# Runs of eight product groups between reductions, in place of four, in a pairwise-interaction kernel

## The chip, the cores and the metric

The kernel runs on one core of a Trainium2 chip. TensorE does the matrix products and writes PSUM, VectorE multiplies, ScalarE copies and applies biases, GpSimd starts gathers, and SyncE starts the large loads. The metric is device time in microseconds (us); lower is better. Before the change the median of three runs is 269.88 us (267.64 to 270.34).

## The reference

512 samples each carry 32 integer ids. Each id picks a row of 64 values from its own table, so a sample becomes 32 vectors of 64. For each of the 496 pairs of fields i < j there is a 64x64 matrix, and the pair's value is a bilinear form:

```
rows, cols = np.triu_indices(32, k=1)
pij = einsum('bpe,dpe,bpd->bp', e[:, rows], kernel, e[:, cols])
z = pij @ W.T + b                                  # 496 -> 256
h = relu(concat([z, dense_ctx]) @ W_top1 + b_top1) # 272 -> 512
h = relu(h @ W_top2 + b_top2)                      # 512 -> 256
y = h @ W_top3                                     # 256 -> 1
```

Everything is fp32.

## The kernel before, in words

**Data.** The 32 fields are paired into 16 chunks. A chunk lies in `x_sb` as 128 partitions (two fields of 64 values) by 512 samples. The rows of the first three chunks are picked with one-hot matrices. For the other 13 GpSimd gathers eight blocks of 128 rows a chunk (L258, 104 gathers in all, each held back until the one two before it has landed, L255 to L257), and TensorE turns each gathered chunk with four transposes (`turn`, L295 to L304, matmuls L303). ScalarE copies the turned chunk out (L450, L454).

**Product groups.** The pair values are made in 124 groups of four pairs. A group's two matmuls multiply the pairs' matrices with a chunk (`products`, L306 to L329). They use 64 rows of the array each (L320, L321), run side by side on the two halves of the array, and fill two PSUM banks of the tensor `t_ps`. As fp32 each appears in the trace as two instructions, so a group is four PE instructions in two slots. VectorE then multiplies the two banks by the other field's vector into SBUF (L507, the buffer `prod`), one instruction a group. `t_ps` holds three groups (`T_RING` = 3, six banks): TensorE may start group g when VectorE has finished group g - 3 (L312, L313).

**Sums over partitions.** What is left of a pair is a sum over 64 partitions. TensorE does it with a selector matrix (`reduce`, L333 to L345, matmuls L341): one `reduce(q)` takes groups 2q and 2q+1, four matmuls side by side on four column strips of the array, each two instructions, so eight PE instructions in two slots. The sums of 16 reduces gather in the one PSUM bank `sum_ps`, and ScalarE keeps a full bank (L436). `reduce(q)` waits until VectorE has finished group 2q+1.

**Order.** TensorE's order is written out in advance. Groups come chunk by chunk (chunk c has c groups), reduces come in bursts: `RUN` says how many groups stand between two bursts. With `RUN` = 4, after each group g with g % 4 == 1, `reduced_after(g)` gives two reduces, those of the groups g - 5 to g - 2. So the cycle is four groups, two reduces. `prod` has `RUN` + 2 = 6 slots, and VectorE may overwrite a slot when its reduce is done (L499, L500). The turn of a chunk c from 7 on stands three groups ahead of its first group, wherever that falls in the run (`plan`).

**Groups inside a chunk pair.** Four of the 124 groups (`WITHIN`) hold pairs whose two fields share a chunk. They use 64x64 quarters of the array, two halves of two slots each (L324, L325, then L328, L329), and the burst of reduces stands between the two halves. They are placed where g % `RUN` == 1: groups 5, 25, 57 and 109.

**End.** After the last group TensorE does the first matrix of the dense layers for three kept banks (L348), the reduces that are left (two), and the dense layers (L373 to L400).

Of the kernel before, what the change touches and what calls it, by code (L numbers as in the profile page):

```python
# [33 lines left out]
FIELD = FIRST_FIELDS + [f for f in range(FIELDS) if f not in FIRST_FIELDS]  # L34
V_ROWS = 125
PER = 10
RUN = 4
OH_RING = 8


# [3 lines left out]
for c in range(CHUNKS):  # L44
    across = [(c, False, [[(i, 2 * c), (i, 2 * c + 1)] for i in (2 * a, 2 * a + 1)]) for a in range(c)]
    within = [(c, True, [[(2 * a + 1, 2 * a), (2 * a + 2, 2 * a + 3)] for a in (c - 3, c - 1)])] if c % SET == SET - 1 else []
    at = (1 - len(GROUP)) % RUN
    GROUP += across[:at] + within + across[at:]
GROUPS = len(GROUP)
# [24 lines left out]
REDUCES = NT // COLS  # L74
# [3 lines left out]
T_RING = 3  # L78
PROD_RING = RUN + 2
G_RING = 8  # L80
# [12 lines left out]
def reduced_after(g):  # L93

    return range(max(0, (g - RUN - 1) // 2), (g - 1) // 2) if g % RUN == 1 else range(0)


def plan():
# [10 lines left out]
def build(nc, ids, ids_t, iota, pick, tables, kern, w_pairs, b_int, ctx_rows, w_ctx_rows, w1, b1, w2, b2, w3, ident, selector, out):  # L109
    steps = plan()  # L110
    with ExitStack() as ctx:
# [156 lines left out]
        def _(pe):  # L268
# [37 lines left out]
            def products(g):  # L306
                c, within, tiles = GROUP[g]
                k = BLOCK_OF[g]
                for s in range(SLICES):
                    if k <= s * KS < k + 1 + within:  # L310
                        pe.wait_ge(k_in[s], 32)
                if g >= T_RING:  # L312
                    pe.wait_ge(prod_ready, g - T_RING + 1)  # L313
                if g == FIRST_GROUP[c]:
                    pe.wait_ge(x_ready, 2 * (c + 1))
                t = t_ps[:, g % T_RING]
                low, high = slice(0, EMB), slice(EMB, P)
                if not within:
                    a = tiles[0][0][0] // 2
                    pe.matmul(t[:, 0, :], k_sb[low, k, :], x_sb[low, a, :], start=True, stop=True)  # L320
                    pe.matmul(t[:, 1, :], k_sb[high, k, :], x_sb[high, a, :], start=True, stop=True).then_inc(t_ready, 1)  # L321
                    return
                a = c - SET + 1
                pe.matmul(t[low, 0, :], k_sb[high, k, low], x_sb[high, a, :], start=True, stop=True)  # L324
                pe.matmul(t[high, 1, :], k_sb[low, k, high], x_sb[low, a + 3, :], start=True, stop=True)  # L325
                for q in reduced_after(g):
                    reduce(q)
                pe.matmul(t[low, 1, :], k_sb[high, k + 1, low], x_sb[high, a + 2, :], start=True, stop=True)  # L328
                pe.matmul(t[high, 0, :], k_sb[low, k + 1, high], x_sb[low, a + 1, :], start=True,  # L329
                          stop=True).then_inc(t_ready, 1)  # L330

            def reduce(q):
                w, k = q // SLOTS, q % SLOTS  # L333
                if q == 0:
                    pe.wait_ge(sel_in, 16)
                pe.wait_ge(prod_ready, 2 * q + 2)
                if k == 0 and w >= 1:
                    pe.wait_ge(window_kept, w)
                for j in range(COLS):
                    t = COLS * q + j  # L340
                    mm = pe.matmul(sum_ps[32 * j:32 * j + 32, :], sel_sb[:, 30 - 2 * k:62 - 2 * k],  # L341
                                   prod[:, (t // 2) % PROD_RING, t % 2, :], start=(k == 0),
                                   stop=(k == SLOTS - 1 or q == REDUCES - 1), tile_position=(0, 32 * j))
                mm.then_inc(prod_used, 1)

            def z_of(m, wins):
                for w in wins:
                    mm = pe.matmul(z_ps[m], w_pairs_sb[:, w, m * P:(m + 1) * P], pair_sums[:, w, :],  # L348
                                   start=(w == 0), stop=(w == WINS - 1))
                return mm  # L350

            spread_ids()
            for kind, n in steps:
                if kind == "fill":
                    if n < ONE_HOTS:
                        pick_rows(n)
                    else:
                        turn(n)
                else:
                    products(n)  # L360
                    for q in reduced_after(n) if n not in WITHIN else ():
                        reduce(q)
# [3 lines left out]
            z_of(0, range(WINS - 1))  # L366
            pe.wait_ge(prod_ready, GROUPS - 2)
            z_of(1, range(WINS - 1))
            for q in range(REDUCES - RUN // 2, REDUCES):
                reduce(q)  # L370
            for n in range(H1 // P):
                rows = slice(32 * n, 32 * n + CTX)
# [31 lines left out]
        def _(act):  # L404
# [36 lines left out]
            for kind, n in steps:  # L441
                if kind == "fill":
                    if n < ONE_HOTS:

                        ahead = len([k for k in BY_ACT if k <= LAST_PICK[n] + OH_RING // 2])
                        one_hots(BY_ACT[made:ahead])
                        made = ahead
                    from_ps = pick_ps[n % 2] if n < ONE_HOTS else tp_ps
                    act.wait_ge(filled, n + 1)
                    act.copy(x_sb[:, n, :], from_ps[:]).then_inc(x_ready, 1)  # L450
                    rows = slice(n % 2 * EMB, (n % 2 + 1) * EMB)
                    if n >= SET and n % SET == 0:
                        act.wait_ge(prod_ready, WITHIN[n // SET - 1] + 1)
                    act.copy(own_sb[rows, n % SET // 2, :], from_ps[rows, :]).then_inc(x_ready, 1)  # L454
                else:
                    for q in reduced_after(n):
                        if q % SLOTS == SLOTS - 1:
                            keep_window(q // SLOTS)
# [122 lines left out]
```

## Time and profile before

| | us |
|---|---|
| median of 3 runs | 269.88 |
| lowest, highest | 267.64, 270.34 |
| the profiled execution | 268.16 |
| its span (first to last instruction) | 266.3 |
| TensorE busy in it | 245.6 (92%) |
| VectorE busy | 171.2 (64%) |

The span is 1.86 us shorter than the execution's own time; what lies around it is not touched here. TensorE's busy time overstates it somewhat where matmuls overlap, since their ends are modelled. A matmul's recorded duration (0.59 us) is longer than the distance to the next one (0.43 us); it is the distance that costs time on TensorE. The weight load (PEld) runs beside matmuls, so idle time of PEld is not idle time of TensorE.

### The profile page before, as it was taken

The page shows a single profiled execution, that of the slowest core. Times are in us where ns is not written, and L with a number is a line of the kernel's source. Part 1 is how long each engine was busy: PE and PEld are TensorE (multiplying, and loading weights), DVE is VectorE, ACT ScalarE, POOL GpSimd, SP SyncE. Part 2 cuts the span into 40 slices and gives each one's busy share as a digit, 9 for nine tenths or more (in the row PEclk, how much of TensorE's full clock was granted, in tenths as well). Part 3 has the DMA queues.
Part 4 walks back from the last instruction along what each step waited for, and adds up shares of the span by engine and source line. Part 5 has one row for each costly group of instructions (what it writes and reads, how often), then busy time and mean ns, then how long its engine had stood idle before and what let it go on. Part 6 is the DMA issues. An engine that isn't in the chain of part 4 may idle for free.

```text
span 266.3 us, 3316 instructions
## 1 busy us (share of the span) xinstructions
PE 245.6 (92%) x1262; PEld 89.1 (33%) x1262; DVE 171.2 (64%) x173; ACT 43.6 (16%) x74; POOL 142.0 (53%) x213
## 2 busy tenths in 40 slices
PE   3999899986769999949999999999999999999996
PEld 1234233322133333312332333333333323333474
DVE  2887746762616687843676878868888858880120
ACT  3686830301010102001010020010100100000121
POOL 4798877768897858376894497888100000000000
PEclk9999999998959999995999999999999999999999
DMA  6541152643131162806019300110000000000000
GB/s 169 173 118 43 25 130 64 161 112 97 22 91 29 28 170 76 197 15 177 20 30 248 76 20 23 24 20 22 10 0 2 0 0 0 4 0 0 2 0 0
DMA packets 9626, 15.97 MB, mean 60 GB/s; under 512 B 3890, under 2 KB 4534, under 8 KB 9610
## 3 DMA queue, kind: packets, MB, share of 16 engines
q1 hardware_dynamic: 6116, 12.32, 17.8%
q0 software_dynamic: 3328, 3.41, 6.0%
q8 instruction: 10, 0.16, 0.3%
q10 hardware_dynamic: 166, 0.02, 0.1%
q14 instruction: 6, 0.05, 0.1%
HBM read 15.75 MB, written 0.00 MB: 59 GB/s over the span
## 4 chain that ended last, share of the span: by engine, by line
PE 54%; DMA 21%; POOL 20%; issue 4%; ACT 0%
PE t_ps L320 27%; DMA gathered<-in_tbl,ids_sb 20%; PE sum_ps L341 15%; POOL gathered L258 14%; POOL rest_sb L265 6%; PE t_ps L380 3%; PE tp_ps L303 2%; PE tp_ps L348 1%; PE t_ps L389 1%; PE t_ps L348 1%; PE t_ps L328 1%; PE t_ps L324 1%; DMA ids_sb<-in_ids 1%; PE tp_ps L389 1%; PE sum_ps L389 1%
## 5 line engine op out<-in xcount | busy, mean ns | idle before, releaser
L507 DVE TENSOR_TENSOR prod<-t_ps,x_sb 128x1024 f32<-128x1024 f32 x120 | 139.9, 1217 | 54.1 <-PE t_ps L321 45.5
L258 POOL DMA_INDIRECT gathered<-in_tbl,ids_sb x104 | 100.0, 961 | 45.1 <-DMA gathered<-in_tbl,ids_sb 28.8
L320 PE MATMUL t_ps<-x_sb,k_sb 64*128 64x512 f32 x240 | 119.6, 632 | 0.8 <-issue 0.4
L321 PE MATMUL t_ps<-x_sb,k_sb 64*128 64x512 f32 x240 | 119.7, 633 | 0.0
L320 PEld LDWEIGHTS t_ps<-x_sb,k_sb 64*128 64x128 f32 x240 | 43.2, 194 | 67.1 <-issue 41.8
L341 PE MATMUL sum_ps<-prod,sel_sb 128*32 128x512 f32 x496 | 60.3, 604 | 0.0
L321 PEld LDWEIGHTS t_ps<-x_sb,k_sb 64*128 64x128 f32 x240 | 43.1, 194 | 0.0
L265 POOL MEMSET rest_sb<- 128x320 f32 x104 | 41.9, 402 | 0.1
L450 ACT COPY x_sb<-tp_ps 128x512 f32<-128x512 f32 x15 | 8.8, 586 | 127.0 <-PE tp_ps L303 75.4
L341 PEld LDWEIGHTS sum_ps<-prod,sel_sb 128*32 128x32 f32 x496 | 13.0, 110 | 43.7 <-issue 24.8
L494 DVE TENSOR_SCALAR k_sb<-ids_bc,iota_sb 125x512 f32<-125x512 f32 x42 | 22.6, 579 | 5.6 <-PE tp_ps L291 2.1
L291 PE MATMUL tp_ps<-k_sb 125*64 125x512 f32 x72 | 20.4, 677 | 1.0 <-ACT k_sb L431 1.0
L303 PE MATMUL tp_ps<-ident_sb,gathered 128*128 128x128 f32 x52 | 9.3, 307 | 11.8 <-DMA gathered<-in_tbl,ids_sb 11.8
L436 ACT COPY pair_sums<-sum_ps 128x512 f32<-128x512 f32 x4 | 2.3, 586 | 68.7 <-PE sum_ps L341 68.7
L303 PEld LDWEIGHTS tp_ps<-ident_sb,gathered 128*128 128x128 f32 x52 | 6.0, 152 | 22.2 <-issue 22.2
L291 PEld LDWEIGHTS tp_ps<-k_sb 125*64 125x64 f32 x72 | 6.0, 156 | 13.7 <-issue 8.6
L507 DVE TENSOR_TENSOR prod<-t_ps,own_sb 128x1024 f32<-128x1024 f32 x4 | 4.9, 1224 | 8.7 <-PE t_ps L329 6.6
L428 ACT ACTIVATE distance<-ids_bc,iota_sb 125x512 f32<-125x512 f32 x12 | 8.6, 717 | 3.6 <-PE tp_ps L291 3.2
L291 PE MATMUL sum_ps<-k_sb 125*64 125x512 f32 x36 | 8.9, 594 | 0.0
L454 ACT COPY own_sb<-tp_ps 64x512 f32<-64x512 f32 x15 | 8.7, 579 | 0.3
L431 ACT ACTIVATE k_sb<-distance 125x512 f32<-125x512 f32 x12 | 7.6, 630 | 0.4
L380 PE MATMUL t_ps<-own_sb,w_sb 128*128 128x512 f32 x16 | 7.1, 599 | 0.0
(47 smaller groups left out, 73.1 us busy)
## 6 DMA issues: line engine op xcount, KB each, us to landing
k_sb<-in_kern SPq DMA_DIRECT2D x32, 256.0 KB, 4.0
gathered<-in_tbl,ids_sb POOLq DMA_INDIRECT x104
w_sb<-in_w SPq DMA_DIRECT2D x2, 512.0 KB
k_sb<-in_tbl SPq DMA_DIRECT2D x3, 280.0 KB
k_sb<-in_tbl SPq DMA_DIRECT2D x3, 224.0 KB
w_pairs_sb<-in_w_pairs SPq DMA_DIRECT2D x1, 512.0 KB
ctx_sb<-in_ctx_rows SPq DMA_DIRECT2D x1, 192.0 KB
w_ctx_sb<-in_w_ctx_rows SPq DMA_DIRECT2D x1, 192.0 KB
```

Of the source, the lines that this page charges most:

```text
L258: pool.indirect_dma_start(gathered[:, n % G_RING, t, f * EMB:(f + 1) * EMB], None, tables[field], bass.IndirectOffsetOnAxis(ap=ids_sb[:, t ...
L265: pool.memset(rest_sb[:], 0.0).then_inc(rested, 1)
L291: mm = pe.matmul(bank[half:half + EMB, :], table_sb[:, f, r, :], one_hot[:, n % OH_RING, :], start=(r == 0), stop=(r == PICK[f][0] - 1))
L303: mm = pe.transpose(tp_ps[:, t * P:(t + 1) * P], gathered[:, n % G_RING, t], ident_sb[:])
L320: pe.matmul(t[:, 0, :], k_sb[low, k, :], x_sb[low, a, :], start=True, stop=True)
L321: pe.matmul(t[:, 1, :], k_sb[high, k, :], x_sb[high, a, :], start=True, stop=True).then_inc(t_ready, 1)
L341: mm = pe.matmul(sum_ps[32 * j:32 * j + 32, :], sel_sb[:, 30 - 2 * k:62 - 2 * k], prod[:, (t // 2) % PROD_RING, t % 2, :], start=(k == 0), ...
L380: mm = pe.matmul(h1_ps[n], w1_sb[:, m, n * P:(n + 1) * P], z_sb[:, m, :], start=False, stop=(m == 1))
L450: act.copy(x_sb[:, n, :], from_ps[:]).then_inc(x_ready, 1)
L454: act.copy(own_sb[rows, n % SET // 2, :], from_ps[rows, :]).then_inc(x_ready, 1)
L494: dve.tensor_scalar(one_hot[:, n % OH_RING, :], ids_bc[:, f, :], iota_sb[:, PICK[f][1] + r:PICK[f][1] + r + 1], None, ALU.is_equal).then_i ...
L507: dve.tensor_tensor(prod[:, g % PROD_RING], t_ps[:, g % T_RING], q, ALU.mult).then_inc(prod_ready, 1)
```

## The change

`RUN` goes from 4 to 8. From it follow:

- eight groups stand between two bursts, and a burst has four reduces, of the groups g - 9 to g - 2, after each g with g % 8 == 1;
- `prod` has 10 slots in place of 6 (40 KB in place of 24 KB of each partition);
- the groups inside a chunk pair stand at 6, 25, 57 and 113; `t_ps` stays at three groups.

The line of the tail that does the last reduces now takes its start from the plan (`REDUCED`). It is 60 for both values of `RUN`, so two reduces are left in both. The numbers of matmuls, of VectorE instructions, of transposes and of loads are the same.

```diff
-RUN = 4
+RUN = 8
 OH_RING = 8
...
 def reduced_after(g):
 
     return range(max(0, (g - RUN - 1) // 2), (g - 1) // 2) if g % RUN == 1 else range(0)
+
+
+REDUCED = max(max(reduced_after(g), default=-1) for g in range(GROUPS)) + 1
...
-            for q in range(REDUCES - RUN // 2, REDUCES):
+            for q in range(REDUCED, REDUCES):
                 reduce(q)
```

The order on TensorE from chunk 10's turn on, before and after. F is a turn, R a burst (with the numbers of its reduces), w a group inside a chunk pair, whose burst stands between its halves:

```
before: F10 44 45 R20-21 46-49 R22-23 50-53 R24-25 F11 54-57w R26-27 58-61 R28-29 62-65 R30-31 F12 66-69 R32-33
        70-73 R34-35 74-77 R36-37 F13 78-81 R38-39 82-85 R40-41 86-89 R42-43 90 F14 91-93 R44-45 94-97 R46-47
        98-101 R48-49 102-104 F15 105 R50-51 106-109w R52-53 110-113 R54-55 114-117 R56-57 118-121 R58-59 122 123
after:  F10 44-49 R20-23 50-53 F11 54-57w R24-27 58-65 R28-31 F12 66-73 R32-35 74-77 F13 78-81 R36-39
        82-89 R40-43 90 F14 91-97 R44-47 98-104 F15 105 R48-51 106-113w R52-55 114-121 R56-59 122 123
```

## Rows read from the trace of the kernel before

**Rows 1.** The page: busy time by engine, and granted TensorE clock in 40 slices.
```profile
PE 245.6 (92%) x1262; PEld 89.1 (33%) x1262; DVE 171.2 (64%) x173; ACT 43.6 (16%) x74; POOL 142.0 (53%) x213
PEclk9999999998959999995999999999999999999999
```

**Rows 2.** The page: product multiply on VectorE and reduce matmuls, busy, mean | idle before.
```profile
L507 DVE TENSOR_TENSOR prod<-t_ps,x_sb 128x1024 f32<-128x1024 f32 x120 | 139.9, 1217 | 54.1 <-PE t_ps L321 45.5
L341 PE MATMUL sum_ps<-prod,sel_sb 128*32 128x512 f32 x496 | 60.3, 604 | 0.0
```

**Rows 3.** Busy time in four stretches: PE, PEld, DVE, ACT, POOL, PEclk, DMA, GB/s.
```profile
115.70:119.30 3.60, 0.05 (x2) 0.03 (x1) 1.59 (x2) 0.00 (x0) 3.16 (x5) 0.90 0.09 18
119.30:125.40 6.10, 6.10 (x20) 2.27 (x24) 2.45 (x2) 1.06 (x2) 4.41 (x8) 0.50 0.64 178
126.60:238.50 111.90, 111.90 (x649) 38.15 (x645) 88.61 (x77) 6.76 (x12) 47.81 (x72) 1.00 0.13 30
161.85:167.34 5.49, 5.49 (x36) 1.88 (x33) 4.62 (x5) 0.00 (x0) 4.61 (x7) 1.00 0.10 21
```

**Rows 4.** TensorE in one cycle, in order of time: start, duration, instruction.
```profile
161.85 0.69 PE L320 MATMUL t_ps<-x_sb,k_sb 64*128 64x512 f32 x1
162.38 0.59 PE L320 MATMUL t_ps<-x_sb,k_sb 64*128 64x512 f32 x1
...
164.31 0.18 PEld L320 LDWEIGHTS t_ps<-x_sb,k_sb 64*128 64x128 f32 x1 [0.44 <-DVE prod L507]
...
164.53 0.59 PE L320 MATMUL t_ps<-x_sb,k_sb 64*128 64x512 f32 x1
...
164.96 0.59 PE L320 MATMUL t_ps<-x_sb,k_sb 64*128 64x512 f32 x1
...
165.49 1.92 PE L341 MATMUL sum_ps<-prod,sel_sb 128*32 128x512 f32 x16
...
167.34 0.69 PE L320 MATMUL t_ps<-x_sb,k_sb 64*128 64x512 f32 x1
```

**Rows 5.** VectorE in order of time: after group 57's second half, and the cycle of Rows 4.
```profile
144.88 1.22 DVE L507 TENSOR_TENSOR prod<-t_ps,own_sb 128x1024 f32<-128x1024 f32 x1 [2.10 <-PE t_ps L329]
146.02 4.60 DVE L507 TENSOR_TENSOR prod<-t_ps,x_sb 128x1024 f32<-128x1024 f32 x4
...
163.03 4.62 DVE L507 TENSOR_TENSOR prod<-t_ps,x_sb 128x1024 f32<-128x1024 f32 x4 [0.87 <-PE t_ps L321]
```

**Rows 6.** TensorE around a turn inside a run, and one behind a burst.
```profile
37.29 0.59 PE L320 MATMUL t_ps<-x_sb,k_sb 64*128 64x512 f32 x1
...
37.82 0.66 PE L303 MATMUL tp_ps<-ident_sb,gathered 128*128 128x128 f32 x4
38.41 0.69 PE L320 MATMUL t_ps<-x_sb,k_sb 64*128 64x512 f32 x1
...
137.53 0.66 PE L303 MATMUL tp_ps<-ident_sb,gathered 128*128 128x128 f32 x4
138.12 0.69 PE L320 MATMUL t_ps<-x_sb,k_sb 64*128 64x512 f32 x1
```

**Rows 7.** A ScalarE copy, and TensorE's restart after waiting for it.
```profile
39.13 0.58 ACT L454 COPY own_sb<-tp_ps 64x512 f32<-64x512 f32 x1
39.85 0.66 PE L320 MATMUL t_ps<-x_sb,k_sb 64*128 64x512 f32 x1 [0.31 <-ACT own_sb L454]
...
40.35 0.59 PE L320 MATMUL t_ps<-x_sb,k_sb 64*128 64x512 f32 x1
```

**Rows 8.** Last gather of chunk 10 (chain), and the second gather behind chunks 11 and 12.
```profile
116.78 2.39 DMA gathered<-in_tbl,ids_sb
...
134.10 0.95 POOL L258 DMA_INDIRECT gathered<-in_tbl,ids_sb  x1 [0.17 <-issue]
...
152.52 0.95 POOL L258 DMA_INDIRECT gathered<-in_tbl,ids_sb  x1 [0.17 <-issue]
```

**Rows 9.** TensorE's turns that waited for a gather (chunks 6, 7, 10), idle before in brackets.
```profile
62.54 0.63 PE L303 MATMUL tp_ps<-ident_sb,gathered 128*128 128x128 f32 x4 [3.83 <-DMA gathered<-in_tbl,ids_sb]
...
75.83 1.08 PE L303 MATMUL tp_ps<-ident_sb,gathered 128*128 128x128 f32 x4 [4.42 <-DMA gathered<-in_tbl,ids_sb]
...
119.30 1.09 PE L303 MATMUL tp_ps<-ident_sb,gathered 128*128 128x128 f32 x4 [3.55 <-DMA gathered<-in_tbl,ids_sb]
```

## The prediction

> **What bounds the kernel now.** I read the busy shares first: TensorE 92%, VectorE 64% [rows 1]. A share over the whole span says little, so next the stretches [rows 3]. From 126.60 to 238.50 us TensorE is busy for all 111.90 us at full clock, VectorE for 88.61: TensorE alone sets the end there. Before that the gathers do: the turns of chunks 6, 7 and 10 found TensorE idle for 3.83, 4.42 and 3.55 us [rows 9], and chunk 10's is released by the last of its gathers, 116.78 + 2.39 = 119.17 [rows 8]. So whatever the change costs or saves before 119.30 is swallowed as long as TensorE still has to wait there, and all of it counts from there on. Then the inside of one cycle, whose means the page gives as 1.217 us a multiply and 0.604 a reduce instruction [rows 2], but whose distances count.
>
> **One cycle in its pieces** [rows 4]. Slots inside the products are 0.43 us apart (164.53 to 164.96), 0.858 a group. Into the burst: 164.96 + 0.43 = 165.39, and the burst is recorded at 165.49, +0.10. The burst holds four slots (1.71) and lasts 1.85 to 167.34, +0.14. The first slot behind it takes 0.53 (161.85 to 162.38), +0.10, its weight load standing bare. 4 x 0.858 + 1.71 + 0.34 = 5.49, the whole cycle [rows 3]. So there are no waits in it, and a change into reduces and back costs **0.34 us**.
>
> VectorE [rows 5]: four multiplies in 4.62 us, one of 1.214 (the page's 1.217) and three steps of (4.62 - 1.21) / 3 = **1.135 us**. TensorE makes a group in 0.858. In a run of products VectorE falls behind by 0.28 a group and recovers in the burst. How near is it to holding TensorE up? The first multiply ends at 163.03 + 1.21 = 164.24, the weight load that waited for it starts at 164.31 [rows 4], 0.07 later, and group 4 of the run could stream another 0.10 later, at 164.41. Its slot is at 164.53. With four groups TensorE escapes by 0.12 us.
>
> **What the change removes.** Of each two bursts one goes, so 0.34 us per eight groups. The reduces themselves are only moved, 62 before and after.
>
> **What it adds.** Groups 5 to 8 of a run meet a `t_ps` that is still three groups deep. Counting from the cycle at 161.85: the second multiply ends at 165.38, so group 5 can stream at 165.38 + 0.17 = 165.55, and its slot would be 165.39: 0.16 lost. From there TensorE goes at VectorE's step: groups 6, 7 and 8 lose 1.135 - 0.858 = 0.28 each. Sum 0.16 + 0.84 = **1.00 us** per run of eight, three times what the removed change of mode gives. VectorE then idles longer in the burst of four (3.43 us), which doesn't help. The restart gap of 0.17 can be read a second time [rows 7]: the copy ends at 39.71, the matmul is recorded at 39.85 and its next slot comes 0.50 later, so streaming began at about 39.92, 0.21 behind the copy. That end would make it 1.04.
>
> The Trainium skill's page "TensorEngine Tiling (Array Packing)" says, under PSUM Bottleneck, that tiling speeds the array up but not the emptying of PSUM, which can then become the bound. The steps of 1.135 against 0.858 show it here.
>
> **A turn inside a run** costs TensorE 37.72 to 38.41 plus a bare weight load, 0.09 + 0.59 + 0.10 = 0.78 [rows 6]; next to a burst it costs 0.59 (137.53 to 138.12), because it shares the changes of mode. In a run that TensorE loses to VectorE anyhow, the turn fills time that would be waited. So each run from chunk 10's turn (119.30) to the end, after against before:
>
> - 44-49: the burst of before fell in slow clock; -0.34, and the groups reach full clock slightly later, together **-0.28**.
> - 50-57: chunk 11's turn now stands inside (+0.19), almost no wait (0.08): **-0.07**.
> - 58-65, behind a half group 57: its multiply at 144.88 holds the next to 146.02 [rows 5], 0.08 later than a free VectorE would start; wait 1.08, so **+0.74**.
> - 66-73: no turn inside. 1.00 - 0.34 = **+0.66**.
> - 74-81: chunk 13's turn now inside, after four groups, +0.19 + 0.22 - 0.34 = **+0.07**.
> - 82-89: **+0.66**.
> - 90-97 and 98-105: the turn is inside in both kernels (behind the first group, and before the last); it leaves waits of 0.16 + 0.28 + 0.28 = 0.72, so **+0.38** each.
> - 106-113: the last group's first half finds a lighter wait, 0.86 in all, **+0.52**.
> - 114-121: as 58-65, **+0.74**.
>
> Sum **+3.80 us**, of which waits +6.76 and changes of mode -2.96. Two groups, two reduces and the dense layers behind that are the same.
>
> **Before 119.30.** From chunk 9's turn the run 34-41 adds as much as 90-97 (+0.38) and the arrival at chunk 9 slips by up to 0.1, so of the 3.55 us in front of chunk 10 about 3.1 stay: covered, cost 0. Without that cover it would be 0.5. Around chunk 6 the burst 4-5 moves behind the turn; 1.85 us more work then stands in front of chunk 7, which waited 4.42 [rows 9]: covered. The groups inside a chunk pair at 6 in place of 5 hold chunk 4's second copy until multiply 6 is done, about 1.1 + 1.2 us, before the wait of chunk 6: covered. Gathers: chunk 10's and all others keep their times, since GpSimd waits only for turns far behind it. Chunk 11's turn comes at about 135.4 instead of 137.53, its gather has landed by 134.10 (the second gather behind it starts then [rows 8]); chunk 12 has landed by 152.52 for a turn at 156. No wait, but only 1.3 us of room at chunk 11. `prod` with ten slots: the next run overwrites what the previous burst has read, as now.
>
> **Sum against the profiled execution:** 268.16 + 3.80 = 271.96. It is 1.72 us below the median of 269.88; with it the four times shown are 267.64, 268.16, 269.88, 270.34, mean 269.0. The differences between them can't come from the stretch that TensorE fills, so they add. I take 269.0 + 3.8 = **272.8 us**; by the median it would be 273.7, by the lowest 271.4.
>
> **Rivals.**
>
> A. *The clock stays up at chunk 10.* From 119.30 to 125.40 the granted clock is 0.50, the 1.2 GHz level, after 3.55 us without matmuls; that costs 6.10 / 2 = 3.05 us [rows 3, 9]. The change shortens that idle time to about 3.1. If the clock then stays at 2.4 GHz, the sum is at best 3.80 - 3.05 = +0.75; chunk 11's gather then binds (turn at about 132.9, landing by 134.0) and VectorE is behind sooner in 44-49, which makes it +1.8: 269.8 to 270.8. For it: chunk 6's turn, after 3.83 us, began at full clock. Against: it fell a little later all the same, and 0.45 us is a small difference. 13%.
>
> B. *TensorE is not held up; the change pays.* This is the other side. Its place is group 5 of each run, its price the 6.76 us of waits, its turning point a VectorE step of about 0.86 to 0.9 in place of 1.135, or a PSUM with room for more than three groups. Then only the changes of mode count: -2.96, 266.0. For it: four groups run without a wait now. Against: with 0.12 us of room, and nothing that speeds VectorE up. 7%. The skill's page "Perfetto Trace Analysis", under Matmul Optimizations, wants matmuls back to back in batches, since the engine's power follows its use; read as a reason for longer runs it gives this case. No row shows a batch of four slowed by being short: the clock is 1.00 through all of 126.60 to 238.50.
>
> C. *The new small waits bring the clock down.* Waits of 0.28 us before each of groups 6 to 8 leave the array less busy. One such fall costs about 3 us by the price at 119.30, on top of 3.8: 275.9 and more, 279 with two. Against: in a waiting run TensorE still streams 0.858 of each 1.135 us, and at 62.54 it took an idle stretch of 3.83 us. 5%. The skill's page "TensorE: Matmul & The Clock Gate" has such a case, under A second HAM failure mode, where small idle times between groups that cycle through PSUM let the clock swing; no run here shows it yet.
>
> D. *Cover is missing.* Chunk 11's gather is later than in this execution by more than its 1.3 us of room, or the waits before chunk 10 count. Bounds: 0.5 for the latter, 2.1 for the former (the turn back at 137.5): +4.3 to +6.4, 273.3 to 275.4. 12%.
>
> The forecast keeps 63%: +3.3 to +4.3, over the spread of the executions 270.9 to 274.6. It has two firm terms, the step and the change of mode, both read from a cycle that repeats.
>
> **How the numbers follow.** A measurement of this kernel tells about 1%, 2.7 us, from no change. The forecast at +3.8 is above that in most outcomes but not by much: of its 63% I give 54 to slower, 9 to within 1%. A is within (13), B faster for most (6) and within (1), C slower (5), D slower (12). Faster 0.06, same 0.23, slower 0.71. The range takes in A's upper part and D, and leaves out B, most of C and the ends: 269.9 to 275.4.
>
> **What would show it.** Right: in a run without a turn, matmuls of groups 6 to 8 start 1.135 us apart instead of 0.858; VectorE's merged stretches hold eight multiplies (9.16 us) with one idle time of some 2.5 us; such a run with its burst lasts 11.6 us instead of 10.98; PE waits "<- DVE prod" appear in front of L320; TensorE's idle time before the turn at 119.3 is near 3.1 us and the granted clock behind it 0.50. A is right if that clock is 1.00, B if the distances stay at 0.858, C if a slice behind 126 us shows a clock below 1.00, D if chunk 11's turn has idle time put down to a gather. I am wrong in the main step if VectorE's step is shorter than 1.135 once it is never starved, or if the wait is released earlier than 0.17 us before streaming.

## The result and the profile after

| | before | after |
|---|---|---|
| median | 269.88 us (9 runs, 267.64 to 271.74) | 271.50 us (9 runs, 270.79 to 272.01) |
| ratio of the two, 95% interval | | 1.0071 [1.0044, 1.0099] |
| the profiled execution, its span | 268.16, 266.3 | 270.79, 269.0 |
| turn of chunk 10 starts | 119.30 | 119.67 |
| from there to the first dense matmul | 119.13 | 121.41 |
| from there to the end | 27.87 | 27.92 |

The change makes the kernel slower: by 0.7% of 269.88, some 1.9 us, by the ratio, and by 1.6 us by the medians. The interval does not contain 1, and the loss is within 1%. The ratios here and below leave disturbed executions out and are not the quotients of the medians beside them; the two differ by up to 0.4 of a per cent (1.2 us, in e9). Between the profiled executions it is +2.7 us of span: 0.37 from a chunk 10 that landed later, 2.28 in the stretch that TensorE fills, 0.05 behind it.

The page after, busy time and granted clock, then the multiply and the reduce matmuls, which answer to [rows 1, 2] (lines are three higher from `REDUCED` on):

```profile
PE 245.3 (91%) x1262; PEld 87.7 (33%) x1262; DVE 170.2 (63%) x173; ACT 43.6 (16%) x74; POOL 141.7 (53%) x213
...
PEclk9999999996899999998999999999999999999999
...
L510 DVE TENSOR_TENSOR prod<-t_ps,x_sb 128x1024 f32<-128x1024 f32 x120 | 138.4, 1215 | 56.5 <-PE t_ps L324 52.1
...
L344 PE MATMUL sum_ps<-prod,sel_sb 128*32 128x512 f32 x496 | 56.5, 595 | 0.0
```

None of these lines shows the loss: TensorE's busy time is 0.3 us *shorter*, although it waits more. The waits are hidden in its modelled ends: a matmul is recorded as 0.59 to 0.69 us where the next comes 0.43 later, so the record covers the first 0.16 to 0.26 us of any wait. Stretches give the sum (columns as in [rows 3]): the slow clock behind chunk 10's turn, the whole stretch, and one run of eight with its burst.

```profile
120.20:123.60 3.40, 3.40 (x9) 1.55 (x10) 1.22 (x1) 1.06 (x2) 2.66 (x4) 0.51 0.64 162
119.67:241.08 121.41, 121.38 (x673) 39.68 (x673) 90.06 (x79) 7.82 (x14) 52.33 (x80) 0.99 0.16 37
167.53:179.13 11.60, 11.60 (x70) 4.15 (x70) 9.14 (x8) 1.17 (x2) 10.07 (x17) 1.00 0.11 21
```

The steps themselves are seen in the order of time. TensorE in the run of groups 82 to 89, from the last slot of group 85 on, answers to [rows 4]:

```profile
182.17 0.59 PE L323 MATMUL t_ps<-x_sb,k_sb 64*128 64x512 f32 x1
182.65 0.18 PEld L323 LDWEIGHTS t_ps<-x_sb,k_sb 64*128 64x128 f32 x1 [0.71 <-DVE prod L510]
182.65 0.69 PE L323 MATMUL t_ps<-x_sb,k_sb 64*128 64x512 f32 x1
...
183.78 0.69 PE L323 MATMUL t_ps<-x_sb,k_sb 64*128 64x512 f32 x1
...
184.91 0.69 PE L323 MATMUL t_ps<-x_sb,k_sb 64*128 64x512 f32 x1
...
186.04 0.69 PE L323 MATMUL t_ps<-x_sb,k_sb 64*128 64x512 f32 x1
...
187.10 3.64 PE L344 MATMUL sum_ps<-prod,sel_sb 128*32 128x512 f32 x32
```

Groups 86 to 89 start 1.13 us apart, at VectorE's step, instead of 0.858. Each begins with its weight load standing bare (0.69 for 0.59), because TensorE waited even for that. VectorE, against [rows 5]:

```profile
144.84 9.13 DVE L510 TENSOR_TENSOR prod<-t_ps,x_sb 128x1024 f32<-128x1024 f32 x8
...
180.24 9.14 DVE L510 TENSOR_TENSOR prod<-t_ps,x_sb 128x1024 f32<-128x1024 f32 x8 [2.47 <-PE t_ps L324]
```

Eight multiplies without a break, then 2.47 us idle in the burst: from the later groups of a run on VectorE sets the pace, in the burst TensorE does. The turns that waited, against [rows 9]:

```profile
104.79 0.63 PE L306 MATMUL tp_ps<-ident_sb,gathered 128*128 128x128 f32 x4 [2.01 <-DMA gathered<-in_tbl,ids_sb]
...
119.67 0.63 PE L306 MATMUL tp_ps<-ident_sb,gathered 128*128 128x128 f32 x4 [1.85 <-DMA gathered<-in_tbl,ids_sb]
```

### The profile page after: what moved, and what is told of

It reads as the page before. It is cut to its first block, busy times and chain, and to the rows that moved or that the text cites. A ratio compares the mean times of both kernels' runs of the same rounds, so it can differ in the third digit from the quotient of the medians.

```text
span 269.0 us, 3316 instructions
## 1 busy us (share of the span) xinstructions
PE 245.3 (91%) x1262; PEld 87.7 (33%) x1262; DVE 170.2 (63%) x173; ACT 43.6 (16%) x74; POOL 141.7 (53%) x213
## 4 chain that ended last, share of the span: by engine, by line
PE 55%; POOL 21%; DMA 19%; issue 4%; ACT 0%
PE t_ps L323 29%; DMA gathered<-in_tbl,ids_sb 19%; POOL gathered L261 15%; PE sum_ps L344 14%; POOL rest_sb L268 6%; PE t_ps L383 3%; PE tp_ps L351 1%; PE tp_ps L306 1%; PE t_ps L392 1%; PE t_ps L351 1%; DMA ids_sb<-in_ids 1%; PE t_ps L327 1%; PE t_ps L331 1%; PE tp_ps L392 1%; PE sum_ps L392 1%
## 5 line engine op out<-in xcount | busy, mean ns | idle before, releaser
L510 DVE TENSOR_TENSOR prod<-t_ps,x_sb 128x1024 f32<-128x1024 f32 x120 | 138.4, 1215 | 56.5 <-PE t_ps L324 52.1
L323 PE MATMUL t_ps<-x_sb,k_sb 64*128 64x512 f32 x240 | 122.6, 633 | 2.5 <-ACT own_sb L457 2.3
L324 PE MATMUL t_ps<-x_sb,k_sb 64*128 64x512 f32 x240 | 122.6, 634 | 0.0
L323 PEld LDWEIGHTS t_ps<-x_sb,k_sb 64*128 64x128 f32 x240 | 40.9, 192 | 75.4 <-issue 41.7
L344 PE MATMUL sum_ps<-prod,sel_sb 128*32 128x512 f32 x496 | 56.5, 595 | 0.0
L324 PEld LDWEIGHTS t_ps<-x_sb,k_sb 64*128 64x128 f32 x240 | 40.8, 192 | 0.0
L344 PEld LDWEIGHTS sum_ps<-prod,sel_sb 128*32 128x32 f32 x496 | 14.5, 109 | 39.8 <-issue 34.7
L497 DVE TENSOR_SCALAR k_sb<-ids_bc,iota_sb 125x512 f32<-125x512 f32 x42 | 23.2, 605 | 4.0 <-ACT ids_bc L415 1.5
L306 PE MATMUL tp_ps<-ident_sb,gathered 128*128 128x128 f32 x52 | 8.8, 294 | 12.8 <-DMA gathered<-in_tbl,ids_sb 12.8
L294 PE MATMUL tp_ps<-k_sb 125*64 125x512 f32 x72 | 19.4, 646 | 1.0 <-ACT k_sb L434 1.0
L306 PEld LDWEIGHTS tp_ps<-ident_sb,gathered 128*128 128x128 f32 x52 | 5.7, 146 | 23.0 <-issue 23.0
L277 PE MATMUL t_ps<-id_rows_h,ident_h 6*125 6x512 f16 x6 | 2.8, 638 | 4.9 <-DVE ident_h L483 4.9
```

The source lines that it names most:

```text
L294: mm = pe.matmul(bank[half:half + EMB, :], table_sb[:, f, r, :], one_hot[:, n % OH_RING, :], start=(r == 0), stop=(r == PICK[f][0] - 1))
L306: mm = pe.transpose(tp_ps[:, t * P:(t + 1) * P], gathered[:, n % G_RING, t], ident_sb[:])
L497: dve.tensor_scalar(one_hot[:, n % OH_RING, :], ids_bc[:, f, :], iota_sb[:, PICK[f][1] + r:PICK[f][1] + r + 1], None, ALU.is_equal).then_i ...
L510: dve.tensor_tensor(prod[:, g % PROD_RING], t_ps[:, g % T_RING], q, ALU.mult).then_inc(prod_ready, 1)
```

## The experiments

Theories: **W**, the loss is TensorE's waits for VectorE, made by three groups of `t_ps` and a step of 1.135 us, less the saved changes of mode. **R**, longer runs, longer bursts or the larger buffer cost something of their own. **C**, the granted clock behind chunk 10's turn takes part. (These three are not the rivals A to D of the prediction.) "Stretch" below is the time from chunk 10's turn to the first dense matmul in the profiled execution, a window whose row is shown (columns as in [rows 3]).

**e1 and e12: the larger buffer alone.**

```diff
-RUN = 8
+RUN = 4
...
-PROD_RING = RUN + 2
+PROD_RING = 10
```

> Runs of four as before, but the buffer of products in SBUF has ten slots instead of six: the memory part of the change alone. The wait theory (the change loses time only where TensorE waits for VectorE because t_ps holds three groups) expects no change, within 0.5 us of before, and the same distances on TensorE. A rival, that the larger buffer itself (its place in SBUF, the looser wait of VectorE on its slots) does something, expects a part of the measured +1.9 us here.

> The kernel with runs of four and ten slots once more. If its gain was a matter of how the clock and the gathers fell in those executions, the median moves toward that of before (within 1 us); if it is a property of the ten slots, it is again 1.5 to 2.5 us below before.

First 266.94 us against 268.82, ratio 0.9908 [0.9872, 0.9945]; again 269.03 against 268.62, ratio 1.0003 [0.9963, 1.0043]. The first result was a miss of the expectation and didn't repeat; the ten runs went from 264.35 to 271.40, so its interval was too narrow. Stretches of the first, of the second, and of ten slots with runs of four at full clock (e11, told below with e7):

```profile
120.18:238.04 117.86, 117.86 (x673) 39.89 (x673) 91.04 (x79) 7.82 (x14) 52.31 (x80) 0.99 0.16 38
```
```profile
122.04:239.91 117.87, 117.87 (x672) 40.15 (x672) 90.98 (x79) 7.82 (x14) 52.34 (x80) 0.99 0.16 38
```
```profile
121.30:237.51 116.21, 116.21 (x672) 39.64 (x673) 90.90 (x79) 7.83 (x14) 52.24 (x80) 1.00 0.17 39
```

The first two agree to 0.01 us, and are 1.26 shorter than before's 119.13. The low clock lies in the first 8 us behind the turn. These 8 us are, in before, in e1 and in e12:

```profile
119.30:127.30 8.00, 8.00 (x32) 2.88 (x34) 2.45 (x2) 1.06 (x2) 5.25 (x9) 0.62 0.52 148
```
```profile
120.18:128.18 8.00, 8.00 (x38) 2.82 (x40) 3.30 (x3) 1.06 (x2) 5.64 (x10) 0.79 0.54 148
```
```profile
122.04:130.04 8.00, 8.00 (x38) 3.06 (x40) 3.29 (x3) 1.06 (x2) 5.45 (x10) 0.79 0.54 148
```

Priced as (1 - clock) times 8.00 us, the low clock cost before 3.0 us and the two others 1.7 us, which leaves 116.1 and 116.2 of work. With the clock at 1.00 six slots (e7, below) and ten (e11) have the same stretch of 116.21 us, to 0.01. So the buffer does nothing on TensorE. What differs is how long the clock stayed low, and when chunk 10 landed: the two profiled executions are 1.86 us apart (267.78 and 269.64), and so are their turns (120.18, 122.04).

**e2: `t_ps` used two groups deep, with runs of four.**

```diff
+DEPTH = 2
...
-                if g >= T_RING:
-                    pe.wait_ge(prod_ready, g - T_RING + 1)
+                if g >= DEPTH:
+                    pe.wait_ge(prod_ready, g - DEPTH + 1)
```

> Runs of four as before, but TensorE starts group g only when VectorE has finished group g - 2 instead of g - 3 (t_ps used two groups deep). The wait theory: group 3 of a run can stream at 164.24 + 0.17 = 164.41 where its slot was 163.67, so it loses 0.74, group 4 another 0.28, 1.02 us a run of four. About twenty runs stand behind chunk 10's turn, so the time goes up by 17 to 21 us, with VectorE's multiplies of a run 1.135 us apart as before. If the depth of t_ps is not what holds TensorE up, the time stays within 3 us of before.

287.16 us against 268.82, ratio 1.0701 [1.0641, 1.0761]. The stretch:

```profile
121.74:257.58 135.84, 126.23 (x675) 36.93 (x673) 94.91 (x81) 7.82 (x14) 51.84 (x79) 1.00 0.14 33
```

The time rose by 18.3 us by the medians, inside the 17 to 21 expected. The stretch is 19.63 us over the 116.21 of e7 at the same clock. In a run, the second half of the array in groups 3 and 4:

```profile
170.32 0.69 PE L324 MATMUL t_ps<-x_sb,k_sb 64*128 64x512 f32 x1 [0.47 <-DVE prod L511]
...
171.44 0.69 PE L324 MATMUL t_ps<-x_sb,k_sb 64*128 64x512 f32 x1
```

Group 3 waits where with three groups nothing does, and here the wait is long enough to show as idle time of PE. The depth of `t_ps` is what decides where waits begin.

**e3 and e4: the waits taken away, by halving the multiply.** The second half of the samples is left out of the result; TensorE's work is the same, since the reduce matmuls read the first half twice.

```diff
-dve.tensor_tensor(prod[:, g % PROD_RING], t_ps[:, g % T_RING], q, ALU.mult)
+dve.tensor_tensor(prod[:, g % PROD_RING, :, 0:HALF], t_ps[:, g % T_RING, :, 0:HALF], q[:, :, 0:HALF], ALU.mult)
...
-                                   prod[:, (t // 2) % PROD_RING, t % 2, :], start=(k == 0),
+                                   prod[:, (t // 2) % PROD_RING, t % 2:t % 2 + 1, 0:HALF].broadcast_to([P, 2, HALF]), start=(k == 0),
```

> Runs of four, and VectorE multiplies only the first 256 of the 512 samples of each bank (the reduce matmuls read these twice, so TensorE's work is unchanged; the second half of the samples is left out of the result). It is the base for the next kernel. Wait theory: TensorE had no waits with runs of four, so the stretch behind chunk 10's turn is as long as before (119.2 us), the time within 0.7 us of before. Were TensorE quietly held up by VectorE already with four, it would be shorter by over 1 us.

> Runs of eight with the same halved multiply (second half of the samples left out). VectorE's step falls to about 0.6 us, below TensorE's 0.858, so no run waits. Wait theory: only the changes of mode count, so the stretch behind chunk 10's turn is 2.9 us shorter than in the kernel with the halved multiply and runs of four at equal clock (1.7 to 3 us shorter in the whole time), and groups 5 to 8 of a run follow each other at 0.858. Rival: the longer runs or bursts cost TensorE something of their own; then it is no faster than that kernel, or slower.

Runs of four: 269.43 us, ratio to before 1.0026 [0.9992, 1.0059]. Runs of eight: 265.17, ratio 0.9896 [0.9840, 0.9951]. Stretches of e3 (its first 8 us, then the whole), then of e4 with its turn of chunk 11 and VectorE inside a run:

```profile
119.25:127.25 8.00, 8.00 (x32) 2.87 (x34) 1.39 (x2) 1.06 (x2) 5.00 (x9) 0.61 0.53 148
```
```profile
119.25:238.37 119.12, 119.12 (x672) 40.77 (x672) 54.66 (x79) 7.82 (x14) 52.27 (x80) 0.97 0.17 38
```
```profile
120.14:234.26 114.12, 113.23 (x672) 41.62 (x672) 54.66 (x79) 7.82 (x14) 52.21 (x79) 1.00 0.17 39
...
134.22 0.63 PE L306 MATMUL tp_ps<-ident_sb,gathered 128*128 128x128 f32 x4 [0.89 <-DMA gathered<-in_tbl,ids_sb]
...
158.97 0.69 DVE L510 TENSOR_TENSOR prod<-t_ps,x_sb 128x512 f32<-128x512 f32 x1 [0.17 <-PE t_ps L324]
159.83 0.69 DVE L510 TENSOR_TENSOR prod<-t_ps,x_sb 128x512 f32<-128x512 f32 x1 [0.17 <-PE t_ps L324]
```

This pair is the heart of the study. With runs of four a VectorE that is busy 36 us less saves TensorE 0.01 us, at a clock that fell as in before (0.61 over the first 8 us, 0.62 there): before, it was held up nowhere. With runs of eight VectorE now waits for TensorE, every 0.86 us, and the stretch is 5.00 us shorter than e3's. Of that 3.05 is clock, by the price of the slow stretch before [rows 3], which e3 matches in length and clock; 1.95 stays, and with the 0.89 us idle at chunk 11, 2.84. The forecast had 2.96 for the changes of mode alone. So R falls, and rival B's mechanism is real: runs of eight pay as soon as VectorE can follow. In the whole time e4 is 4.3 us below e3 by the medians, more than the 1.7 to 3 expected, since the low clock was gone altogether (1.00, after 1.18 us of idle time at chunk 10).

**e5 and e6: other lengths.** `RUN = 6` and `RUN = 2`, the rest as after.

> Runs of six, bursts of three reduces, eight slots. Wait theory: a run of six without a turn waits 0.16 + 0.28 = 0.44 us and saves a third of the changes of mode (0.34 per twelve groups), +0.54 per twelve groups against runs of four. A burst of three now falls before chunk 10's turn, which shortens the idle time there to about 1 us. Counted through from chunk 6 that gives +0.6 us at the clock of before, and -0.2 us if the slow stretch behind chunk 10's turn disappears: -0.5 to +1.0, between before and after. Rival: the loss is not from waits but grows with the burst or the buffer, then about half of the change's +1.9.

> Runs of two, one reduce each, four slots. The theory has no waits for VectorE here, but twice the changes of mode: 0.34 us more per four groups, +5.6 us at the clock of before, +2.7 if the slow stretch at chunk 10 disappears (less idle time is left there). It is slower than before by 2.5 to 6 us. If the change of mode were not what a short run costs, it would equal before.

Runs of six: 268.91 against 268.66, ratio 1.0012 [0.9974, 1.0051]. Runs of two: 272.54, ratio 1.0174 [1.0112, 1.0236]. The stretch of e5 with two of its waits, and the stretch of e6:

```profile
120.23:239.71 119.48, 117.25 (x664) 39.09 (x665) 90.38 (x79) 7.85 (x14) 52.21 (x80) 1.00 0.16 38
...
134.21 0.63 PE L306 MATMUL tp_ps<-ident_sb,gathered 128*128 128x128 f32 x4 [1.23 <-DMA gathered<-in_tbl,ids_sb]
...
157.79 1.07 PE L344 MATMUL sum_ps<-prod,sel_sb 128*32 128x512 f32 x8 [0.80 <-ACT pair_sums L439]
```
```profile
120.57:243.30 122.73, 122.73 (x672) 36.15 (x672) 93.82 (x80) 7.82 (x14) 52.35 (x80) 1.00 0.16 37
```

The time of e5 lies where both the theory (-0.5 to +1.0) and its rival (about +0.95) allow it, so it doesn't decide between them. Its trace shows a cost that the theory had left out: bursts of three don't divide the 16 reduces of a bank of sums, so a burst that crosses into a new bank waits 0.80 us for ScalarE to keep the full one. With 1.23 us at chunk 11 that makes 2.03 of the 3.27 us by which this stretch is longer than e7's 116.21 at the same clock; 1.24 are left for everything else.

In e6 the stretch is 6.52 us longer than e7's. By the kernel's own order one more reduce falls into it (with `RUN` = 2, `REDUCED` is 61 and one reduce is left for the end), 0.86 us. That leaves 5.66 us, where 5.6 was expected at equal clock. The groups' last slot, the burst and the next run are

```profile
238.87 0.59 PE L323 MATMUL t_ps<-x_sb,k_sb 64*128 64x512 f32 x1
239.39 1.07 PE L344 MATMUL sum_ps<-prod,sel_sb 128*32 128x512 f32 x8
240.39 0.69 PE L323 MATMUL t_ps<-x_sb,k_sb 64*128 64x512 f32 x1
```

239.39 - 238.87 - 0.43 = 0.09 in, 240.39 - 239.39 - 0.86 = 0.14 out, and the bare load: the same prices as in [rows 4], paid twice as often. By the medians the lengths 2, 4, 6, 8 stand at about +3.9, 0, +0.2 and +1.6 us. Four and six can't be told apart by their times, and VectorE can follow without a wait only up to four.

**e7 and e8: the clock.** Matmuls whose result is thrown away fill TensorE's idle time in front of the turn; `FILL` is {10: 3} with runs of four, {9: 2, 10: 2} with runs of eight.

```diff
+                for _ in range(FILL.get(c, 0)):
+                    pe.matmul(tp_ps[:], ident_sb[:], x_sb[:, 0, :], start=True, stop=True)
                 for rows in rows_in:
```

> The kernel before (runs of four), with three matmuls whose result is thrown away put in front of the wait at chunk 10's turn, so TensorE streams for 2.6 us of the 3.55 it was idle. Clock theory: the granted clock behind 119.3 stays at or near 1.00 and the 3.05 us lost there come back: -2 to -3 us where the slow stretch was, against the kernel before. Rival: the clock falls anyway or costs nothing, within 0.7 us of before.

> The changed kernel (runs of eight) with two thrown-away matmuls each in front of the waits of chunk 9's and chunk 10's turns, 1.7 us of the 2.0 and 1.85 it was idle. Clock theory: the slow stretch of some 3.4 us behind chunk 10's turn goes, -1.7 us at TensorE; chunk 11's gather may then bind, so 0.5 to 1.7 us faster than the changed kernel. And with the clock equal in both, runs of eight against runs of four (the kernel with three such matmuls) show the sum of waits and changes of mode alone: +3.8 in the forecast, +4.9 if chunk 11's gather binds. Rival: the change's net of +1.9 us is all waits and mode, then it stays at +1.9.

> Runs of four with ten slots of products and three thrown-away matmuls in front of chunk 10's wait. The ten slots alone measured 0.9% faster, with times from 264.35 to 271.4, which the theory did not expect. If they help by way of the clock (a shorter slow stretch behind chunk 10), nothing is left to gain here and the time equals that of the matmuls with six slots, 267.0. If they help by something else (the place of buffers, gathers that land earlier), it is 1 to 2 us below that.

Runs of four: 267.03 against 268.66, ratio 0.9952 [0.9920, 0.9984]. Runs of eight: 270.14, ratio 1.0068 [1.0040, 1.0096]. With ten slots and runs of four (e11): 267.25 against 268.62, ratio 0.9968 [0.9935, 1.0001], as with six slots. Stretches of e7, and of e8 with its turn of chunk 11:

```profile
121.40:237.61 116.21, 116.21 (x673) 39.62 (x673) 90.95 (x79) 7.82 (x14) 52.33 (x80) 1.00 0.17 39
```
```profile
121.44:241.85 120.41, 120.00 (x673) 38.98 (x673) 90.11 (x79) 7.82 (x14) 52.37 (x80) 1.00 0.16 37
...
135.41 0.63 PE L309 MATMUL tp_ps<-ident_sb,gathered 128*128 128x128 f32 x4 [0.36 <-DMA gathered<-in_tbl,ids_sb]
```

C holds: the clock is 1.00 throughout, and e7's stretch is 2.92 us shorter than before's. At equal clock the change costs 120.41 - 116.21 = 4.20 us, 0.36 of it at chunk 11, 3.84 for waits and mode; the sum said 3.80.

In the times less arrives. Only 1.6 us of e7's 2.9 are in the medians, between e7 and e8 they show 3.1, and e8 is a miss: 0.5 to 1.7 us faster than the changed kernel was expected, and against its own base it stands where that stood (1.0068 and 1.0071). The traces show where the rest may have gone: chunk 10's turn starts at 121.40, 121.44 and 121.30 in e7, e8 and e11, at 119.30 in before. For e7 and e8 the thrown-away matmuls are not the cause of most of it, since their gathers were late already at chunk 6, far ahead of the first such matmul:

```profile
64.94 0.82 PE L309 MATMUL tp_ps<-ident_sb,gathered 128*128 128x128 f32 x4 [4.13 <-DMA gathered<-in_tbl,ids_sb]
```

That is e7, 2.40 us behind before's 62.54 [rows 9], and e12, without such matmuls, had its turn at 122.04. Why the gathers land at other times from one execution to the next stays open.

**e9 and e10: the idle time used.** Turn 10 one group and turn 11 two groups ahead of their first groups, with runs of four and of eight.

```diff
+LEADS = {10: 1, 11: 2}
...
-        while chunks < CHUNKS and (chunks < max(2, ONE_HOTS) or g >= FIRST_GROUP[chunks] - min(LEAD, (chunks - 1) // 2)):
+        while chunks < CHUNKS and (chunks < max(2, ONE_HOTS) or g >= FIRST_GROUP[chunks] - LEADS.get(chunks, min(LEAD, (chunks - 1) // 2))):
```

> Runs of four, with the turn of chunk 10 one group and that of chunk 11 two groups ahead of their first groups instead of three. Groups 44 and 45 and the burst 20-21, all ready before chunk 10's gather lands, then fill the 3.55 us that TensorE stood idle, and the clock has no reason to fall. Counted through with the arrivals of the trace of before, the end comes 3.5 to 3.7 us earlier (2.7 if all gathers from chunk 9 on come 2 us later): 2.5 to 4 us faster than before, and 0.5 to 2 us faster than the kernel with three thrown-away matmuls. Rival: the stretch is limited by the next gather (chunk 11, landing by 134), so that little more than the 1.6 us of the thrown-away matmuls is gained.

> The changed kernel (runs of eight) with the same two later turns. Two groups move in front of the wait, but the burst does not (it comes only after group 49). Counted through, 0.9 to 1.8 us faster than the changed kernel, and 4.5 to 6 us slower than the same turns with runs of four: the waits and changes of mode keep their price whatever is done about chunk 10. Rival: with later turns the waits of runs of eight are covered by gathers, then the two differ by less than 3 us.

Runs of four: **264.60 us against 268.62**, ratio 0.9894 [0.9847, 0.9941], faster than both kernels. Runs of eight: 270.49, ratio 1.0108 [1.0055, 1.0161]. TensorE around chunk 10 in e9, and its turn of chunk 11:

```profile
117.77 1.92 PE L345 MATMUL sum_ps<-prod,sel_sb 128*32 128x512 f32 x16
...
119.62 0.66 PE L307 MATMUL tp_ps<-ident_sb,gathered 128*128 128x128 f32 x4
...
133.76 0.63 PE L307 MATMUL tp_ps<-ident_sb,gathered 128*128 128x128 f32 x4 [1.00 <-DMA gathered<-in_tbl,ids_sb]
```

The burst 20-21 runs up to the turn at 119.62, which follows without idle time, and the clock behind it is 1.00. The stretches of e9 and e10:

```profile
119.62:233.79 114.17, 112.99 (x653) 38.53 (x649) 89.03 (x78) 7.83 (x14) 52.27 (x80) 1.00 0.16 39
```
```profile
119.83:239.57 119.74, 118.37 (x664) 38.36 (x664) 89.65 (x79) 7.82 (x14) 52.39 (x80) 1.00 0.16 38
```

The two kernels are 5.9 us apart by their medians, at the upper end of the 4.5 to 6 expected, and 5.57 in the stretch. Of that 1.71 are the two reduces that e9 does in front of the turn and e10 behind it, and 0.16 more idle time at chunk 11 (1.16 against 1.00). The 3.70 left are again the waits and changes of mode, near the 3.84 of e7 and e8.

But e10 is no faster than the change itself was against its own base (1.0108 against 1.0071), where 0.9 to 1.8 us of gain were expected: a miss. Two of its six executions show the gain (268.50 and 269.29, the profiled one). The two slowest (271.52 and 271.72) had a mean granted clock of 0.974 and 0.975, the others 0.987; so in these the clock stayed low for longer somewhere, which the one trace, at 0.987, can't show.

## Why the prediction was right

- **The number.** 271.50 us lies inside the range of 269.9 to 275.4, but the middle of it, +3.8 us, came out at +1.6 to +1.9, and "slower by more than 1%", which had 0.71, did not come; within 1% had 0.23. That the time is in the range is partly luck: its lower end was put there for rival A, whose condition, a clock of 1.00 behind chunk 10, did not come true. What was right is the mechanism.
- **The bound** was read rightly: TensorE's records fill the stretch behind chunk 10's turn (121.38 of 121.41 us; the short waits lie under them), and the 0.5 us that the run 34-41 adds before it disappears in the wait for chunk 10.
- **VectorE's step and the wait.** Forecast 1.135 us and 1.00 us a run; measured 1.13, and 11.60 us for a run with its burst against 5.49 x 2 = 10.98, +0.62 where +0.66 was said. TensorE restarts 0.16 us behind VectorE, where 0.17 was said (group 83's multiply ends at 182.59, the weight load follows at 182.65 and stands bare for 0.10). One sign that was named did not show: no wait of PE for VectorE stands in front of the product matmuls. It appears on the weight load alone (0.71 at 182.65), as the waits are too short to leave PE idle.
- **The change of mode** at 0.34: e4 finds 2.84 of 2.96 us, e6 the same pieces.
- **The sum** +3.80: 3.84 at equal clock (e7, e8). It is the term that the whole forecast hung on, but that the two agree so closely is luck. Run 44-49 was counted at -0.28 for a burst in slow clock, and e7 and e8 have no slow clock. The bursts behind group 49, in e7 and in e8, start at

  ```profile
  129.36 1.06 PE L347 MATMUL sum_ps<-prod,sel_sb 128*32 128x512 f32 x8
  ```
  ```profile
  127.78 2.78 PE L347 MATMUL sum_ps<-prod,sel_sb 128*32 128x512 f32 x24
  ```

  which is 7.96 and 6.34 us behind their turns. e7 has done two more reduces by then, 1.71 us, so this run costs 6.34 + 1.71 - 7.96 = +0.09. The other nine come to 3.84 - 0.09 = +3.75, where the list adds up to +4.08. Too little in one and too much in the others cancel.
- **The clock** was the term mis-sized. I priced it at no change, and kept "it stays up" as rival A. It did neither: it fell as before, to 0.51, but for 3.40 us instead of 6.10. Before that cost 3.05, after 3.40 x 0.49 = 1.67, so 1.38 came back, and 3.80 - 1.38 = 2.42 stands against 2.28 measured. That is why +3.8 came out as +2.6 in the profiled execution. Why it is only +1.6 to +1.9 over all executions stays open: before's profiled execution was 1.72 us below its median, after's 0.71. The mean granted clock orders the executions only weakly: of 71 of the kernel before that stand beside the experiments, the 18 with 0.962 took 269.4 us on average, the 26 with 0.968 268.2 and the 27 with more 268.5. How long the clock stays low isn't set by the idle time alone: e1 waited 3.40 us at chunk 10 and lost about as little as after with 1.85.

  ```profile
  120.18 0.63 PE L306 MATMUL tp_ps<-ident_sb,gathered 128*128 128x128 f32 x4 [3.40 <-DMA gathered<-in_tbl,ids_sb]
  ```

- **The gathers** did not keep their times, though I had said that they would: chunk 9's had landed by 103.09 in before and was waited for until 104.79, and chunk 6's was waited for until 64.19 instead of 62.54. Why is not known. It cost nothing at the end but split the idle time over two turns, 2.01 and 1.85 us, where one of 3.1 was forecast. Chunk 11 did not bind in the change itself (turn at 134.63 without idle time), but it held TensorE up in e8 (0.36 us), e4 (0.89), e9 (1.00), e10 (1.16) and e5 (1.23): rival D's room of 1.3 us was as thin as it looked.
- **Rival B** failed on its condition, not its price. **Rival C** didn't come: with waits of 0.28 us in every run the clock is 1.00 from 126.60 on. So the case in the Trainium skill's page "TensorE: Matmul & The Clock Gate", A second HAM failure mode, is not met by waits this short in this kernel. The rule of the Trainium skill's page "Perfetto Trace Analysis", Matmul Optimizations, to run matmuls back to back in batches, gave nothing here beyond the changes of mode.
- **The level.** I set 269.0 as the middle of four executions; the median of nine is 269.88, and the 271.50 measured is 1.62 above it.

## What to carry to other kernels

Two engines that alternate through a buffer of n tiles can be unequal in speed without cost only for a limited number of tiles in a row: the lag grows by the difference of their steps with each tile, and the run should end where it reaches the buffer's depth. Work that out from start-to-start distances in one cycle, since busy shares (64% for the engine that decides) and recorded idle times hide it. Look also at what else a run's length must divide: bursts of three waited for ScalarE at a bank of 16 reduces, the other lengths did not. And before saving tenths per cycle behind a wait, look at what could stand in front of it: two groups and a burst moved ahead of one gather were worth 4.0 us by the medians and 2.8 by the ratio, more than this change lost.

## What was not expected of the hardware

- A matmul's record runs 0.16 us past the start of the next slot, so waits up to about 0.26 us leave no idle time on PE, and the busy time fell while waits rose (245.6 to 245.3).
- The same program's executions differ by up to 7 us with nothing changed (264.35 to 271.40 in e1), enough for an interval that excluded 1 around a change that does nothing on TensorE.
- After idle times of 3.55 and 3.33 us at chunk 10 (before, e3) TensorE's clock stayed at its lower level, 1.2 GHz, so long that the first 8 us were at 0.62 and 0.61. After 3.40, 3.46 and 1.85 us (e1, e12, after) they were at 0.79. After 1.18, 0.74 and 0.57 us (e4, e6, e5) the clock was 1.00. The idle time alone doesn't order these: 3.33 us cost more than 3.46.
- The same gathers land up to 2.7 us apart in different executions: chunk 10's turn waited for its gather until 119.30 in before and until 122.04 in e12.
